# The last group by halves, and another order at the first groups: a GNN layer and a routed FFN on one core

## The reference

```
h   = layernorm(x)
a   = relu(bn(conv1d(relu(bn(conv1x1(h))), 17 taps)) + h)   # over the nodes
s   = h @ w_se.T + b_se                                      # 3 values for each node
nmp = (exp(-|s_i - s_j|^2) * adj) @ relu(h @ w_msg.T + b_msg)
r, z, n = gates of a GRU on [a, nmp] and h
x   = x + (1 - z) * n + z * h
h2  = layernorm(x);  w = h2 @ wr + br
sel = the 511 nodes of each batch with the largest w
y   = (gelu(h2[sel] @ w1 + b1) @ w2 + b2) * w[sel]           # 128 -> 512 -> 128
out = x + h2, and y added to the rows in sel
```

## Time and profile before

| | |
|---|---|
| three runs | 562.45 to 562.78, median 562.78 |
| the profiled execution | 561.96, of it 560.1 span |
| TensorE busy | 544.9 (97%), 2964 matmul passes |
| VectorE, ScalarE, GpSimd busy | 475.0 (85%), 355.2 (63%), 276.1 (49%) |
| granted TensorE clock | 0.999 in the mean |

### The profile page before, as it was taken

One profiled execution on the slowest core, in us unless ns is written; L12 is line 12 of the kernel. 1 busy time (PEld: TensorE's weight loads), 2 busy tenths in 40 slices (PEclk: granted clock), 3 DMA queues, 4 the chain that ended last, 5 costly groups with the idle time before them and its releaser, 6 DMA issues.

```text
span 560.1 us, 9036 instructions
## 1 busy us (share of the span) xinstructions
PE 544.9 (97%) x2964; PEld 414.8 (74%) x2964; DVE 475.0 (85%) x1056; ACT 355.2 (63%) x617; POOL 276.1 (49%) x346
## 2 busy tenths in 40 slices
PE   7899999999999999999999999999999999989996
PEld 4876798678967896689767986798678966755663
DVE  7997388689898989899999989898979987988722
ACT  5867485856586667748674857575856673645552
POOL 3640354325358444834484546654545265437552
PEclk9999999999999999999999999999999999999999
DMA  8703700270008200750057001800171005402102
GB/s 276 280 0 80 297 0 2 71 305 1 2 11 294 109 2 1 208 207 1 1 136 278 1 2 54 323 2 1 46 282 49 1 1 180 160 12 85 38 33 62
DMA packets 33340, 54.53 MB, mean 97 GB/s; under 512 B 2098, under 2 KB 23051, under 8 KB 33166
## 3 DMA queue, kind: packets, MB, share of 16 engines
q1 hardware_dynamic: 29710, 48.42, 24.8%
q0 software_dynamic: 3584, 5.54, 2.9%
HBM read 44.21 MB, written 13.43 MB: 103 GB/s over the span
## 4 chain that ended last, share of the span: by engine, by line
PE 81%; DVE 11%; issue 3%; ACT 3%; POOL 1%; DMA 0%; DVEq 0%; ACTq 0%; POOLq 0%
PE N L1548 19%; PE M L1525 10%; PE C L1381 7%; PE C L1382 6%; PE C L1383 6%; PE D L1519 5%; PE N L1642 4%; PE N L1381 3%; PE N L1382 3%; PE N L1383 3%; ACT hab L681 2%; PE M L1382 2%; PE M L1381 2%; PE M L1383 2%; DVE tr L1036 2%
## 5 line engine op out<-in xcount | busy, mean ns | idle before, releaser
L787 ACT ACTIVATE tr<-D 128x512 f32<-128x512 f32 x128 | 76.4, 597 | 75.6 <-PE D L1519 73.9
L1525 PEld LDWEIGHTS M<-cst,adjb 128*128 128x128 f32 x512 | 63.8, 141 | 35.5 <-issue 20.8
L1519 PE MATMUL D<-V,U 128*128 128x512 f32 x128 | 89.3, 698 | 0.7 <-DVE V L1095 0.7
L1525 PE MATMUL M<-cst,adjb 128*128 128x128 f32 x512 | 76.8, 272 | 0.6 <-DVE ga L1127 0.6
L581 POOL DMA_INDIRECT sel<-R,ridx x56 | 61.1, 1090 | 16.0 <-issue 13.8
L1548 PE MATMUL N<-ga,msgF 128*128 128x512 f32 x128 | 64.2, 593 | 0.0
L1548 PE MATMUL N<-tz,msgF 128*128 128x512 f32 x128 | 64.2, 593 | 0.0
L1381 PE MATMUL C<-zR,wc 128*128 128x256 f32 x208 | 60.6, 291 | 0.1
L1382 PE MATMUL C<-zR,wc 128*128 128x256 f32 x208 | 58.6, 282 | 0.0
L1383 PE MATMUL C<-zR,wc 128*128 128x256 f32 x208 | 58.5, 281 | 0.0
L1157 DVE TENSOR_SCALAR_CACHE_REDUCE junk<-W,R 128x1024 bf16<-128x1024 f32 (+3 forms) x64 | 51.7, 808 | 3.7 <-ACT W L749 3.7
(11 more groups left out here) (245 smaller groups left out, 1523.9 us busy)
## 6 DMA issues: line engine op xcount, KB each, us to landing
adjb<-in_adj SPq DMA_DIRECT2D x8, 4096.0 KB, 14.9
adjb<-sel SPq DMA_DIRECT2D x7, 516.0 KB, 5.3
xall<-in_x SPq DMA_DIRECT2D x7, 512.0 KB, 5.3
out<-R SPq DMA_DIRECT2D x7, 512.0 KB, 3.6
R<-in_conv_w SPq DMA_DIRECT2D x1, 1088.0 KB, 7.1
sel<-R,ridx POOLq DMA_INDIRECT x56, 3.5
xall<-in_weights SPq DMA_DIRECT2D x1, 832.0 KB, 9.8
xall<-in_x SPq DMA_DIRECT2D x2, 256.0 KB, 2.8
```

The costliest lines, as they stand in the source:

```text
L787: nc.scalar.activation(E[:, u % NE, :], Db[u % NH][:, :], ACT.Exp, scale=-1.0).then_inc(exp_ok, 1)
L1519: MM(Db[h][:, :], U[:, t * P:(t + 1) * P], V[:, half(h)], start=True, stop=True).then_inc(d_ps, 1)
L1525: i = TR(Mb[h][:, k * P:(k + 1) * P], adjb[:, h * TH + k, t * P:(t + 1) * P], ident)
```

## The change

Three edits. In the last group TensorE makes the second layer for columns 0 to 255 into N0, then for columns 256 to 511 into N1; the transposes, `update`, the rows and the stores follow by halves (two rows each, into M0 and M1). At the start of phase two `sel_to_features(1)` stands ahead of `down(0, 0)`; VectorE makes the blend ahead of rank tile 7 and the indices, and `lo_of_sel(2)` ahead of `moments2`, where it stood at the beginning of step 1. In batch 0 the fronts of tiles 0 and 1 stand ahead of taps 7 and 9 instead of 3 and 7.

```
+EARLY_0 = {7: 0, 9: 1, 11: 2}
...
 # SyncE
-            for h in range(NH):
-                ts = slice(h * TH, (h + 1) * TH)
-                sp.wait_ge(O_ok, TH * (NXS + h + 1))
+            for ts, rows in ((slice(0, TH), TH), (slice(TH, TH + 2), TH + 2), (slice(TH + 2, T), T)):
+                sp.wait_ge(O_ok, TH * NXS + rows)
                 sp.dma_start(out_v[B - 1][:, ts], R[:, 1, ts, D:2 * D]).then_inc(last_out, 16)
...
-            sp.wait_ge(last_out, 16 * NH)
+            sp.wait_ge(last_out, 16 * 3)
...
 # ScalarE
+            def last_update(k):
+                wait(act, y_ps, NG - 1, 1, k + 1)
+                wait(act, yb_ps, NG - 3, 1, 1)
+                cs = slice(k * Q, (k + 1) * Q)
+                nc.scalar.activation(Y[:, 0, cs], Nb[k][:, 0:Q], ACT.Identity, bias=col(V_F2)).then_inc(y_ok, 1)
...
-            update(NG - 1, (NG - 1) % 2)
+            last_update(0)
+            last_update(1)
...
 # VectorE
-            def last_rows(b, h):
-
-                wait(dve, yb_ps, b, 1, 1)
+            def last_rows(b, h, k=None):
+
+                wait(dve, yb_ps, b, 1, 1 + (k or 0))
                 dve.wait_ge(base_ok, B)
                 dve.wait_ge(kept_ok, 1)
-                for c in range(TH):
+                for c in range(TH) if k is None else (2 * k, 2 * k + 1):
                     t = h * TH + c
                     base = R[:, 1, t, D:2 * D]
-                    STT(base, M0[:, c * P:(c + 1) * P], kept[:, t:t + 1], base, ALU.mult, ALU.add).then_inc(O_ok, 1)
+                    back = (M1 if k else M0)[:, c * P:(c + 1) * P]
+                    STT(base, back, kept[:, t:t + 1], base, ALU.mult, ALU.add).then_inc(O_ok, 1)
...
                     new_gate(B - 1, 1)
                     rank(B - 2, 0, 6)
                     lo_of_sel(1, 1)
+                    blend(B - 1, 1)
                     rank(B - 2, 0, 7)
                     indices(B - 2, 0, 1)
-                    blend(B - 1, 1)
                     state_to_nodes(B - 1, (M1, N1))
+                    lo_of_sel(2, 0)
                     moments2(B - 1)
                     mean_and_variance(1, stats2, T * B, slice(0, T), NH)
-                elif not last:
+                elif b > 1 and not last:
                     lo_of_sel(b + 1, 1 - q)
...
-            updated_rows(NG - 1, (NG - 1) % 2)
+            last_rows(NG - 1, 1, 0)
+            last_rows(NG - 1, 1, 1)
...
 # TensorE, conv_odd
-                        if n in EARLY:
-                            front(b, EARLY[n])
+                        early = EARLY_0 if b == 0 else EARLY
+                        if n in early:
+                            front(b, early[n])
...
+            def last_down(k, j):
+                if k == 0:
+                    wait(pe, g_ok, NG - 1, HT, j + 1)
+                    if j == 0:
+                        wait(pe, y_ok, NG - 3, 1, 1)
+                elif j == 0:
+                    wait(pe, y_ok, NG - 2, 1, 1)
+                i = MM(Nb[k][:, 0:Q], wf2[:, j, :], g[0][j][:, k * Q:(k + 1) * Q], start=j == 0, stop=j == HT - 1)
+                if j == HT - 1:
+                    i.then_inc(y_ps, 1)
+
+            def last_back(k):
+                wait(pe, O_ok, NG - 1, TH, 0)
+                wait(pe, y_ok, NG - 1, 1, k + 1)
+                for c in (2 * k, 2 * k + 1):
+                    i = TR((M0, M1)[k][:, c * P:(c + 1) * P], Y[:, 0, c * P:(c + 1) * P], ident)
+                i.then_inc(yb_ps, 1)
+
+            def last_group():
+                b = NG - 1
+                up(b, 0, HT - 1)
+                for j in range(HT):
+                    last_down(0, j)
+                    if j == 1:
+                        update_back(b - 1, 1)
+                for j in range(HT):
+                    last_down(1, j)
+                    if j == 1:
+                        last_back(0)
+                last_back(1)
...
             def ffn_step(b, q, first, last):
+                if last:
+                    last_group()
+                    return
...
-                    elif not last and not (first and j == 1):
+                    elif not (first and j == 1):
                         up(b + 1, 1 - q, j - 1)
-                    down(b, q, j)
                     if first and j == 0:
                         sel_to_features(1)
+                    down(b, q, j)
...
-            update_back(NG - 1, (NG - 1) % 2)
```

## The result

Eight runs of the changed kernel: 564.04 to 565.23, median 564.68, against 562.78 before (eight runs, 562.15 to 563.50). Ratio 1.0034, 95% interval 1.0026 to 1.0043: **slower by 1.9 us**. Predicted were 562.2 and "same", in a range from 560.6 to 563.5; rival (b), the clock, had 563.9 to 564.6. The profiled execution took 564.94, of it 562.7 span.

What follows compares the result with a forecast made beforehand. TensorE was taken to bound the kernel (81% of the chain that ended last, VectorE 11%). Terms -1.17 (tail), +0.58 (first groups) and +0.04 (batch 0) summed to -0.55, giving 562.2 on the median, "same", range 560.6 to 563.5.

Steps and rivals of the forecast that it cites:

- rival (b): First groups: TensorE's clock falls in its 3.5 us wait for the weight column, giving 563.9 to 564.6; chance 0.1.
- the forecast: Whole kernel: the three parts sum to -0.55, giving 562.2 on the median, called "same"; chance 0.58 together with rival (d)'s case.
- The tail's term (-1.17): Last group by halves: 0.72 saved in compute and 0.45 in the last store, bounds -0.72 to -1.28.
- rival (c): Tail and first groups: halves bring only -0.72, reordering costs its upper bound +1.2, giving 563.3; chance 0.12.
- Part 2: First groups' reordering: moments 0.58 late, weight column wait grows to 3.5 us, all behind it late; +0.58, bounds 0 to +1.2.
- the blend-first head start: First groups: VectorE's work runs ahead, 1.5 by the time it meets group 2's low part, and the 0.90 `gn` wait goes.
- Part 3: Batch 0: TensorE's wait moves to tap 4; 0.2 delay mostly covered at the fifth front's transposes, leaving +0.04.

Runs made afterwards that it cites:

- e5: Changed kernel with 12 extra thrown-away products filling TensorE's wait for the weight column: 562.86, ratio 1.0007 to the kernel before.
- e2: Kernel before with only the changed order of the first groups on TensorE and VectorE: 564.39, 1.93 above the kernel before, ratio 1.0035.
- e1: Kernel before with only the tail changed (last group by halves, three stores): 562.50, 0.04 above the kernel before, ratio 0.9999.
- e4: Changed kernel with group 2's low part put back behind the moments, at the start of step 1: 560.71, ratio 0.9969 to the kernel before.
- e3: Kernel before with only batch 0's fronts moved (table `EARLY_0`): 563.14, 0.09 above the kernel before, ratio 1.0002.
- e0: Kernel before, unchanged, run once more for a second trace: 563.40, span 561.5.

## Why the prediction was wrong

**The step that failed** is the choice between the forecast and rival (b). The forecast said that TensorE would arrive at the weight column at 502.5 and "its 0.46 becomes 3.5 us"; measured 3.5. It said that the moments would be 0.58 late; measured from the mark they were 0.41 late, and e5's time agrees (0.40, within a wide interval). It then let the work behind the wait keep its duration and gave the clock a chance of 0.1, because no fall stood in the trace. The mechanism of (b), its place and its direction were right: the clock fell right behind the wait, in the profiled execution and in e2's. In the changed kernel's eight runs the mean clock is 0.994 to 0.997; in the profiled executions without the fall it is 0.998 to 1.000, and single runs of the kernel before also have 0.997, so for one of the eight the mean doesn't tell. The price was 1.5 (e5), where I gave 1.7 to 2.4 and the stretches show 1.7 of clock lost; the intervals of the medians are too wide to tell 1.5 from 1.7. That the time, 564.68, came so near to (b)'s 563.9 to 564.6 is in part luck: (b) still had the tail's -1.17 in it, which did not come.

The Trainium skill, TensorE: Matmul & The Clock Gate, Part 1, states this fall after idleness. By that rule, which I had beside the rival, the trace agrees: 1.00 before the wait, 0.50 behind it. That the trace of before showed no fall was no evidence, since behind the 2.0 at its start it held no wait longer than 0.9.

**The tail's term (-1.17) was right in size and not on the path.** This is the second step that failed. Compute: predicted 0.72 saved, measured 6.56 - 5.86 = 0.70. Store: predicted 0.45 less, measured 2.31 to 1.84 between its issue and SP's wait, 0.47, which bears out the row's 291 GB/s. The Trainium skill, DMA: Bandwidth & Descriptors, Anatomy of one DMA, has the data at 436 GB/s, in a fit for transfers that GpSimd issues, while this store is SyncE's; the estimate of 0.30 worked out from it is less than the 0.47 measured, and the measurement decides. The passes of 256 columns took 0.86 for four and 1.73 for eight, 0.22 each, as taken; ScalarE's halves took 0.48. What was wrong is the sentence that "each part of a microsecond there is one of the span". I had followed the chain to the last instruction that is shown, and the last 2.8 us of the span behind the last store's issue I put down to that store. GpSimd's end, 7.96 behind its last scatter, stood 0.1 behind SP's in the kernel before (559.96 against 559.84), so all of the term went to nothing (e1), and rival (c), which had a smaller tail, named the wrong reason for it.

**Part 2** apart from the clock: the wait for `gn` went, VectorE stood 1.62 (predicted 1.5), the blend-first head start was there and was thrown away by one instruction. I had all the numbers for what e4 shows, and forecast the change as it stood. That TensorE "can't make it up" held: from 524 to 548 it is busy all the time in both, and from 516 to 524 it has 7.42 of 8 us, with a wait of 0.58 for a low part at 518.30, where before it had 8.00.

**Part 3** (+0.04) was right: e3 gives 0.09 within its interval, and the wait moved to tap 4. The 0.2 of delay was covered, as the 0.44 of the fifth front's transposes shows.

The sum by what was measured: +1.5 clock, +0.4 late moments, 0 tail, 0 batch 0 = +1.9, the measured difference of the medians. The split into 1.5 and 0.4 is e5's, so that the two add up says nothing by itself; e2 (+1.93 without tail and batch 0), e1 and e3 are what bears it out. Of the 2.5 between 562.2 and 564.7 the clock made 1.5 and the tail 1.2, less 0.2 by which the moments were less late. The tail alone would have left the time just inside the stated range, the clock alone just outside. The two profiled executions differ by 2.6 in their spans instead, because that of before was 0.7 early; the prediction had noted that it lay 0.8 under the median, and a second trace of it (e0) would have said so.

## What to carry to other kernels

When an edit lets TensorE run ahead of something it must wait for anyway, the gain turns into one long wait, and that can cost more than several short ones: put the work that feeds the fixed point first on the engine that makes it, and the work that only feeds TensorE's run-ahead behind it or in that engine's own idle time. Before shortening a tail, list when each queue ends, GpSimd's included, and not only the chain to the last compute instruction; with two ends a tenth apart both must move. Take a second trace of the kernel before, when the terms are under a microsecond.

## What the runs showed of the hardware

- After a wait of 3.5 us TensorE's granted clock was 0.50 from 508 to 510 (changed kernel, and in e2); after waits of 0.5 to 0.9 in this phase it stayed at 1.00 (kernel before), and with the same wait filled by 12 products (3.04 us) too (e5). The fall cost 1.5 us.
- The wait on GpSimd at the program's end is over 7.96 us behind its last indirect scatter in all 11 traces in which SyncE did not end later, although such a scatter's own issue takes 0.97, its data land 2.3 behind it, and SyncE's store lands 1.8 to 2.3 behind its issue. I did not try what part of GpSimd's end this time belongs to.
- A store of 128 KB in runs of 512 bytes landed 0.47 sooner than one of 256 KB (1.84 against 2.31, issue to SP's wait).
- The start of one and the same kernel varied by 0.33 in when the first x landed, and by 0.7 in when it reached its 488th microsecond (kernel before, two traces).
